# The experts' table of a sparse layer: comparing and marking by groups of eight tiles

## The reference, cut to what matters

```python
def _L1_ffn_ref(hidden_states, gate_w, gate_up_proj, down_proj):   # top 2 of 8 experts
    probs = jax.nn.softmax(x @ gate_w.T, axis=-1)
    w, idx = jax.lax.top_k(probs, TOP_K)
    w = w / jnp.sum(w, axis=-1, keepdims=True)
    ...
    acc = acc + ce[:, None] * (jax.nn.silu(g) * u @ dn.T)
def _L2_ffn_ref(x, shared_w1, shared_w2, experts_w1, experts_w2, gate_w):   # top 2 of 8, and a shared expert
    shared = jnp.einsum('th,hd->td', jax.nn.silu(shared), shared_w2.T)
    ...
    return (shared + selected).reshape(B, S, D)
```

## Time and profile before

| | |
|---|---|
| median of 3 runs | 3520.39 us (3518.59 to 3526.02) |
| profiled execution, its own time | 3524.75 us |
| its span in the trace | 3522.9 us |
| mean granted TensorE clock | 0.932 of full speed |
| the four tables (from the first lanes, L791, to the first read, L801) | 22.3, 22.3, 22.8 and 22.4 us |

### The profile page before, as it was taken

How to read it: one execution, slowest core, us unless ns; L and a number is a source line. 1 busy time by engine, 2 the same in 40 slices (tenths; PEclk the granted TensorE clock), 3 DMA queues, 4 the chain that set the end, 5 groups by cost and what they waited for, 6 DMA issues and landing times. The chain is left out here.

```text
span 3522.9 us, 62960 instructions
## 1 busy us (share of the span) xinstructions
PE 3013.2 (86%) x21353; PEld 1948.5 (55%) x21353; DVE 2406.2 (68%) x6525; ACT 2049.6 (58%) x3059; POOL 1153.8 (33%) x1213
## 2 busy tenths in 40 slices
PE   4669999787758967999999869879778968997999
PEld 3533333344547962222222359859756956886787
DVE  7778888476876558999999475573286335656565
ACT  4459989664532335999999723344344435654565
POOL 4442311121547742001000077557636750001000
PEclk9879999998778988999999979989989989999999
DMA  1041210000011123001000121221202121001000
GB/s 59 1 132 59 70 50 22 1 1 25 1 72 34 49 75 108 21 21 30 21 21 12 44 105 49 67 96 53 73 21 69 52 87 66 1 1 39 31 10 13
DMA packets 80308, 155.00 MB, mean 44 GB/s; under 512 B 21872, under 2 KB 40112, under 8 KB 77696
## 3 DMA queue, kind: packets, MB, share of 16 engines
q1 hardware_dynamic: 59184, 105.08, 9.1%
q0 software_dynamic: 20816, 45.91, 4.5%
HBM read 102.09 MB, written 48.23 MB: 43 GB/s over the span
## 5 line engine op out<-in xcount | busy, mean ns | idle before, releaser
L2590 ACT ACTIVATE core_pr<-core_two 128x1024 f32<-128x1024 f32 (+3 forms) x896 | 787.5, 934 | 47.5 <-PE core_two L2557 43.8
L2626 DVE TENSOR_REDUCE core_mx<-core_one 128x1 f32<-128x512 f32 x778 | 491.4, 684 | 20.4 <-PE core_one L2509 13.0
L2569 PE MATMUL core_ps_o<-core_pr,core_vals 128*32 128x512 f32 (+3 forms) x3584 | 433.9, 559 | 1.7 <-ACT core_oT L2601 1.5
L2509 PE MATMUL core_one<-arena,queries 64*128 64x512 bf16 (+3 forms) x1472 | 374.6, 363 | 29.0 <-PEq L62 19.7
L2557 PE MATMUL core_two<-queries,arena 64*128 64x512 bf16 (+3 forms) x1792 | 340.8, 360 | 9.5 <-ACT core_pr L2590 6.8
L2509 PEld LDWEIGHTS core_one<-arena,queries 64*128 64x128 bf16 x1472 | 113.2, 94 | 296.0 <-DVE core_mx L2626 132.2
L2443 POOL COPY core_vals<-arena 128x288 f32<-128x288 f32 x32 | 14.7, 460 | 782.4 <-PE core_ps_o L2569 782.4
L2620 DVE CUSTOM_DVE_ANT_0 core_junk<-core_one,core_over 128x512 bf16<-128x512 f32 (+4 forms) x334 | 201.7, 644 | 26.6 <-PE core_one L2509 21.9
L585 PE MATMUL moe_first_bank<-moe_first_xrT,moe_first_chosen_w 128*128 128x128 f32 x1704 | 217.0, 278 | 2.3 <-DVE moe_first_xrT L830 2.2
L585 PE MATMUL moe_second_bank<-moe_second_xrT,moe_second_chosen_w 128*128 128x128 f32 x1704 | 215.5, 277 | 2.0 <-DVE moe_second_xrT L830 1.9
L585 PEld LDWEIGHTS moe_first_bank<-moe_first_xrT,moe_first_chosen_w 128*128 128x128 f32 x1704 | 204.6, 194 | 4.4 <-DVE moe_first_xrT L830 4.2
(11 more groups left out here) (637 smaller groups left out, 7170.2 us busy)
## 6 DMA issues: line engine op xcount, KB each, us to landing
arena<-expert_out SPq DMA_DIRECT2D x64, 256.0 KB, 3.7
expert_rows<-arena SPq DMA_DIRECT2D x13, 512.0 KB, 3.0
q_parts<-qkv_parts SPq DMA_DIRECT2D x16, 384.0 KB, 2.6
k_parts<-qkv_parts SPq DMA_DIRECT2D x16, 384.0 KB, 3.5
queries<-q_parts SPq DMA_DIRECT2D x64, 96.0 KB
arena<-k_parts SPq DMA_DIRECT2D x64, 96.0 KB
moe_first_w_up<-in_m_up SPq DMA_DIRECT2D x3, 2048.0 KB, 8.6
moe_second_w_up<-in_m_up SPq DMA_DIRECT2D x3, 2048.0 KB, 9.7
```

The costliest lines, as they stand in the source:

```text
L2509: pe.matmul(one[bank[e]][:, 0:width], q_sb[rows, hq, pair, qt * P:(qt + 1) * P], k_sb[rows, hq, pair, kc * CW:kc * CW + width], start=True ...
L2569: mm = pe.matmul(ps_o[h * 32:(h + 1) * 32, off:CW], vals[:, hq % 2, j, h, :], pr[:, (n * N2 + k) % KEPT, h // 2, h % 2, off:CW], start=(j ...
L2590: a.activation(pr[:, step % KEPT, i, :, off:CW], two[spot[e] % 2][:, :, off:CW], ACT.Exp, scale=HD ** -0.5).then_inc(s_wide, 1)
L2626: v.tensor_reduce(at, scores, AX.X, ALU.max).then_inc(s_read, 1)
```

## The change

The group's work is cut differently over the engines:

- VectorE compares the slots of all eight tiles in one `tensor_tensor` (bf16 slot numbers against f32 `hi`, both spread by broadcast, 568 columns) into a new tile `hits`; makes the lanes of the first five tiles in another (640 columns, bf16 against f32); and multiplies `hits` by the numbers 8n+1 to 8n+8, read from the bf16 slot numbers, in a third (568 columns, both operands bf16, the second a broadcast). These take the place of thirteen instructions.
- GpSimd makes the lanes of the last three tiles (`ALONE`), not of four.
- ScalarE makes the token half, `hits` times the partition number, in one activation of 568 columns. It waits for `hits` (`s_first`) and, from group 2 on, for the products of group n-2. TensorE waits for it with a new semaphore (`s_tokens`). In ScalarE's order it stands at the head of group n, ahead of that group's copy, silu and normalising.

```diff
-    OTHERS = (1, 3, 5, 7)
+    s_aside, s_tokens = st.sem("lanes_aside"), st.sem("tokens")
+    ALONE = range(5, GT)
@@ gpsimd
-                for k in OTHERS:
+                for k in ALONE:
@@ tensor
                 pe.wait_ge(s_cells, n + 1)
+                pe.wait_ge(s_tokens, n + 1)
@@ scalar
-            if shared:
-                for n in range(GROUPS_T * TOPK):
-                    if n in TURNED_AT:
-                        copy_xn(4 + TURNED_AT.index(n))
-                    if n + 1 < GROUPS_T * TOPK:
-                        always(ASIDE)
-                    if n < GT // 2:
-                        normalise(3, range(2 * n, 2 * n + 2))
+            for n in range(GROUPS_T * TOPK):
+                if n >= 2:
+                    a.wait_ge(s_table, n - 1)
+                a.wait_ge(s_first, n + 1)
+                a.activation(cells[:, n % 2, :, SLOTS:2 * SLOTS], hits[:, n % 2], ACT.Identity, scale=r.token).then_inc(s_tokens, 1)
+                if shared and n in TURNED_AT:
+                    copy_xn(4 + TURNED_AT.index(n))
+                if n + 1 < GROUPS_T * TOPK:
+                    always(ASIDE)
+                if shared and n < GT // 2:
+                    normalise(3, range(2 * n, 2 * n + 2))
@@ vector
-                for k in range(GT):
-                    j = n * GT + k
-                    if k not in OTHERS:
-                        v.tensor_scalar(lanes[:, n % 2, k, :], r.laneb[:], lo[:, j:j + 1], None, ALU.is_equal)
-                    last = v.tensor_scalar(cells[:, n % 2, k, 0:SLOTS], r.slotb[:], hi[:, j:j + 1], float(j + 1), ALU.is_equal, ALU.mult)
-                last.then_inc(s_first, 1)
+                group_n = slice(n * GT, (n + 1) * GT)
+                few = slice(n * GT, n * GT + ALONE[0])
+                v.tensor_tensor(hits[:, n % 2], r.slotb[:].unsqueeze(1).to_broadcast([P, GT, SLOTS]),
+                                hi[:, group_n].unsqueeze(2).to_broadcast([P, GT, SLOTS]), ALU.is_equal).then_inc(s_first, 1)
+                v.tensor_tensor(lanes[:, n % 2, 0:ALONE[0]], r.laneb[:].unsqueeze(1).to_broadcast([P, ALONE[0], P]),
+                                lo[:, few].unsqueeze(2).to_broadcast([P, ALONE[0], P]), ALU.is_equal)
                 v.wait_ge(s_first, n + 1)
-                v.tensor_scalar(cells[:, n % 2, :, SLOTS:2 * SLOTS], cells[:, n % 2, :, 0:SLOTS], 0.0, r.token, ALU.is_gt, ALU.mult).then_inc(s_cells, 1)
+                v.tensor_tensor(cells[:, n % 2, :, 0:SLOTS], hits[:, n % 2], r.slotb[:, n * GT + 1:(n + 1) * GT + 1].unsqueeze(2)
+                                .to_broadcast([P, GT, SLOTS]), ALU.mult).then_inc(s_cells, 1)
```

More of the change, by code:

```diff
@@ L334, in sparse_stage @@
     count, inc, over, step = scratch("count", E, T), scratch("inc", E, T), scratch("over", E, T), scratch("step", SLOTS, 7)
+    hits = st.sb("hits", [P, 2, GT, SLOTS], BF16)
     tops = st.sb("tops", [P, TOPK, T])
@@ L374, in sparse_stage @@
     s_scaled = st.sem("scaled")
-    s_aside = st.sem("lanes_aside")
-    OTHERS = (1, 3, 5, 7)
+    s_aside, s_tokens = st.sem("lanes_aside"), st.sem("tokens")
+    ALONE = range(5, GT)
     s_first, s_pair, s_sum = st.sem("cells_first"), st.sem("pair"), st.sem("sum")
```

## The result

| | before | after |
|---|---|---|
| median of 6 runs each, the two kernels on one chip | 3520.7 us (3518.59 to 3531.34) | 3550.65 us (3548.95 to 3554.02) |
| profiled execution, its own time | 3524.75 us | 3550.62 us |
| its span | 3522.9 us | 3548.8 us |
| the four tables | 22.3, 22.3, 22.8, 22.4 | 26.1, 26.1, 32.6, 31.3 |

The ratio after to before is 1.0081, 95% interval 1.0067 to 1.0094. The kernel became 0.8% slower. The forecast was slower by 0.23%, and 3550.65 lies outside its range of 3517 to 3540.

The account below looks back on a forecast made before the run. Operand makers VectorE and GpSimd bound the gated tables, TensorE nearly the shared ones. Losing 12.1 us in the shared and saving 3.9 in the gated adds 8.2 us: 3528.6 us, 0.23% slower, range 3517 to 3540.

Parts of the forecast that it names:

- What bounds the kernel: Four tables: operand makers VectorE and GpSimd pace the gated, TensorE nearly the shared; each delays the end one for one.
- VectorE's three instructions: VectorE's part of a table group: three long instructions at 1.04 ns a column, 2.08 us a group.
- The hold of 0.1 us on VectorE: In each table group, GpSimd's reads delay VectorE by 0.1 us each, three to a group, making 2.38 us.
- GpSimd fits in, one lane tile for each VectorE instruction (0.6 in 0.77 to 0.84): In each table group, GpSimd's three lane tiles of 0.6 us fit beside VectorE's three instructions.
- Each gated table: The two tables of the gated stages: 20.33 us against 22.30, 2.0 saved in each, 3.9 in both.
- the third rival: In the tables, GpSimd and VectorE exclude each other for most of an instruction: 3541 to 3560 us; chance 0.13.
- ScalarE's ring: Shared tables: tokens wait behind silu and normalising, these behind TensorE's products; seven steps 25.15 us, 5.8 and 6.2 lost.
- The start of the shared tables: Group 0 of each shared table: products start near 2334.6 instead of 2334.48, 0.1 us lost in each.
- The sum: Whole kernel: 12.1 us lost in shared tables less 3.9 saved in gated, 8.2 us more, 3528.6 us.
- The first: Rival for the shared tables: ScalarE takes the tokens for nothing, giving 3516.5 down to 3511.6 us; chance 0.12.
- second: Rival for the gated tables: VectorE is quicker than priced, by 0.3 us a group, giving 3523.8 us; chance 0.08.
- The fourth, TensorE's clock: Rival for the shared tables: TensorE's clock falls as its share drops, 21 us in 14 steps, 3550 us; chance 0.07.

Follow-up runs that it names:

- experiment 6: The kernel before, with only the lanes divided anew: three tiles for GpSimd, five for VectorE in short instructions; ratio 1.0014.
- Experiment 1: The changed kernel, with VectorE making all eight lane tiles in one instruction of 1024 columns and GpSimd none; ratio 1.0033.
- 7: The changed kernel with tokens marked a group early and VectorE's five lane tiles made by five short instructions, GpSimd keeping three; ratio 1.0007.
- 8: The changed kernel with tokens marked a group early, one lane tile on GpSimd and seven in one VectorE instruction; ratio 0.9977.
- 9: The changed kernel with tokens marked a group early, two lane tiles on GpSimd and six in one VectorE instruction; tables together 92.3 us.
- experiment 2: The changed kernel, with ScalarE marking the tokens of group n+1 ahead of group n's copy, silu and normalising; ratio 1.0056.
- experiment 5: The changed kernel with all eight lane tiles in one VectorE instruction, none on GpSimd, and tokens marked a group early; ratio 0.9990.
- experiment 4: The changed kernel with all lanes on VectorE, plus four unused GpSimd instructions of 128 columns per group; one execution, no total time given.
- experiment 3: The changed kernel, with the token half made by VectorE in one more instruction after `hits` instead of by ScalarE; ratio 1.0052.

## Why the prediction was wrong, step by step

**What bounds the kernel** was right in its main point: only the four tables moved, and each moved the end one for one (26.2 of 25.9 us). That the two makers of the operands in the gated tables were nearly in balance stood in the earlier trace rows, but was not used; experiment 6 shows it.

**VectorE's three instructions** were right: 0.75, 0.82 and 0.74 us with no GpSimd beside them (forecast 0.75, 0.82, 0.75), the third, one of whose bf16 operands is a broadcast, at the same rate.

**The hold of 0.1 us on VectorE** was right: an instruction in which a lane tile gets through is longer by 0.08 to 0.10 (902 against 818 ns, 833 to 839 against 741). Where the tile ran first, with no VectorE instruction beside it, the price was 0.13: L795 at 1061.98 took 0.88 in place of 0.75, and the tile kept its 0.60.

**"GpSimd fits in, one lane tile for each VectorE instruction (0.6 in 0.77 to 0.84)"** is the step that failed. I had read from the earlier trace rows that GpSimd waits for the end of a VectorE instruction, and then costed only what that does to VectorE. GpSimd's own time I left at 0.6 to 0.8. A lane tile in fact takes 1.4 to 1.8 us beside these three, since it waits for the end of two of them and ends about 0.4 after the second. Three such tiles make 4.7 us against VectorE's 2.2, and only VectorE's pause for want of a buffer lets GpSimd catch up. Each gated table: forecast 2.0 saved, measured 3.8 lost, 5.8 between them. By its parts: the first products come 4.83 us after the start, 2.1 later than in the earlier trace rows and 2.3 later than the sum had room for (20.33 less 1.16 less seven steps), and the seven steps take 20.10 where 7 x 2.38 = 16.7 was forecast, 3.4 more. Experiment 1 shows it by leaving GpSimd out, 7 by short VectorE instructions, 8 and 9 by the number of tiles. The earlier trace rows had the start of the price in them: L2668 took 0.4 us more for a single VectorE end. The form with a scalar by partition had no row beside a long instruction, and for it I bounded only the hold, not the wait. The bound, and the 2.63 us set against the third rival, came from a table whose VectorE instructions are short and have one tensor input, so they said nothing of a lane tile's wait beside long ones with two.

**ScalarE's ring** was right, to 0.08 us a step. One turn in the first shared table, with a turn of four tiles, to be held against the earlier trace rows:

```profile
2349.99 0.67 PE L558 MATMUL moe_first_bank<-arena 128*128 128x142 bf16 x8 [0.96 <-ACT arena L673]
...
2351.99 0.60 ACT L650 ACTIVATE moe_first_h_all<-moe_first_bank 128x512 f32<-128x512 f32 x1 [0.26 <-PE moe_first_bank L524]
...
2352.49 0.86 ACT L635 ACTIVATE arena<-x,moe_first_shift,moe_first_ln_rstd 128x128 f32<-128x128 f32 x2
2353.26 0.76 ACT L673 ACTIVATE arena<-moe_first_hits,route_table 128x568 bf16<-128x568 bf16 x1
...
2354.16 0.35 PE L558 MATMUL moe_first_bank<-arena 128*128 128x142 bf16 x3 [1.31 <-ACT arena L673]
```

Products to silu 2.00 (2.01 forecast), silu to normalising 0.50, tokens at 2353.26, and the next products 0.14 after their end, where 0.04 was put for the hand-over. The steps of the second shared table are 3.79, 4.17, 4.17, 3.78, 3.01, 3.40 and 3.40, 25.72 together; the forecast was 25.15. This is the ring by itself: with GpSimd out (experiment 1) it keeps that length, and with the tokens early (2, 5) it is gone.

**The start of the shared tables** was forecast 0.1 us late and is 2.1 late: 5.09 us after `lo` is begun, where it was 2.99, again by the lane tiles of group 0, while ScalarE's tokens are ready at 2342.84 and the products start at 2344.90. The sentence that VectorE and GpSimd are hidden below the ring holds for the later groups and not for this one.

**The sum.** Forecast 8.2, measured 26.2. The 18.0 between them: gated tables 3.8 lost in place of 2.0 saved, twice, 11.5 (unrounded); start of the shared ones 4.0; the ring's hand-over 14 x 0.08 = 1.1; and 1.3 for the clock, next.

**The rivals.** The first and second did not come. The third was right in its sign and in its price for the gated tables (26.3 us; they are 26.1), and not in how: it had VectorE held for 0.35 us a tile, and VectorE was held for about 0.09, while GpSimd waited 0.8 to 1.2 us inside each slow tile. That the two prices agree is chance. Its total, 3541, was still short of 3550.65, since it too left the start of the shared tables out. With the lock of the Trainium skill ("SBUF — State Buffer", section "Who interferes with whom") the trace agrees for one side: a GpSimd instruction that comes second stands still until VectorE's ends (0.15 to 0.41 us before its own end in experiment 4). For the other side it doesn't: VectorE, coming second, lost 0.08 to 0.13 us to the scalar forms and 0.20 to the product (L802 0.94 against 0.74), and not GpSimd's whole 0.6. The pair in the earlier trace rows, where a longer GpSimd product cost VectorE 0.73 of 0.87 us, stays nearer the lock, and no run here says what makes the difference. The fourth, TensorE's clock, came in one of the two shared tables. Its windows in the first, columns as in the earlier trace rows:

```profile
2341.50:2344.90 3.40, 0.00 (x2) 0.01 (x1) 3.40 (x6) 1.34 (x3) 3.40 (x4) 1.00 0.00 0
2344.90:2347.50 2.60, 2.60 (x10) 1.65 (x11) 1.63 (x3) 0.00 (x0) 2.60 (x4) 0.52 0.01 3
```

TensorE stood idle for 3.40 us waiting for group 0's lanes, and was granted 0.52, about the 1.2 GHz level, for the next 2.60 us: eight products took 1.09 in place of 0.67, and the first step 5.09 where the second table has 3.79. In the second shared table TensorE was idle for 3.25 us at the same place and kept 1.00; in experiment 2 the same 3.25 us there were followed by 0.52. So the wait alone doesn't tell whether the clock will fall. From 2349.9 on the clock was 1.00 again, with ring steps of up to 4.17 us.

**Where the expected gain went.** The gain of merged instructions is real and small: VectorE's group shrinks, and with both losses taken away (experiment 5) the tables are 3.0 us under those before. Both losses come with its two side moves. The lanes left to GpSimd beside long instructions cost 26.2 us less 10.9 (experiment 1) = 15.3, and the place of the tokens in ScalarE's order 26.2 less 16.7 (experiment 2) = 9.5; taken away together they give 29.2, more than the sum, because in the shared tables each hides part of the other.

## What to carry to other kernels

When VectorE's work is merged into fewer and longer instructions, look at what GpSimd does beside it. Ask how long GpSimd's instruction will take as well as what it does to VectorE, and whether the long ones read SBUF alone. Here 0.60 us became 1.4 to 1.8, and giving GpSimd one tile of eight instead of three turned a loss of 3.8 us in each gated table into a gain of 1.6. Work moved to an engine with idle time goes into that engine's order: follow who waits for the instruction ahead of it, and if that leads back to the mover, it is a ring, which shares of busy time don't show.

## What the runs showed of the hardware

- A GpSimd tensor_scalar of 128 columns whose scalar is read by partition takes 0.60 us with VectorE idle, 1.4 to 1.8 (2.13 at most, in experiment 4) beside two-input VectorE instructions of 0.74 to 1.3 us back to back, 0.67 beside short ones, and 0.60 inside one of 0.68 us that takes one of its two inputs from PSUM (experiment 4). Copy (0.29 alone), comparison with a constant (0.54) and product (0.39) wait for one end (experiment 4).
- VectorE's tensor_tensor takes 0.74 us for 568 columns, 0.82 for 640, 1.08 for 896 and 1.22 for 1024, so (1.22 - 0.74) / 456, some 1.05 ns, for each further column. With all operands bf16, one of them a broadcast, it is no quicker than with an f32 operand (0.74 against 0.75).
- VectorE's tensor_scalar of 568 bf16 columns into bf16 takes 0.37 us in the kernel before (L795, median) and 0.47 in experiment 3, where a lane tile gets through in each; the tensor_tensor takes 0.74.
